# A channel-mixing stage whose GpSimd passes move to TensorE, ScalarE and VectorE

## The reference

```python
a4 = att.reshape(b, l, H, S)
m = jnp.mean(a4, axis=-1, keepdims=True)
var = jnp.mean((a4 - m) ** 2, axis=-1, keepdims=True)
att = ((a4 - m) * jax.lax.rsqrt(var + EPS)).reshape(b, l, E) * gn_w + gn_b
x = x + att * g @ Wo.T
xn2 = _ln(x, ln2_w, ln2_b)
sx2 = _token_shift(xn2, state[:, i0])
xk = xn2 + sx2 * ffn_maa_k
xr = xn2 + sx2 * ffn_maa_r
rr = jax.nn.sigmoid(xr @ ffn_Wr.T)
kk = jnp.square(jax.nn.relu(xk @ ffn_Wk.T))
x = x + rr * (kk @ ffn_Wv.T)
```

## Time and profile before

| what | value |
|---|---|
| time, median of 3 runs | 5353.01 us (5352.04 to 5363.05) |
| profiled execution | 5354.71 us, its span 5352.7 us |
| mean granted TensorE clock | 0.946 |
| busy over the span | PE 4758.5, DVE 3731.0, ACT 2930.4, POOL 2071.8 us |
| the changed stage | from 1351.5 to 1746, 394.5 us |

### The profile page before, as it was taken

How to read it: one execution, slowest core, us unless ns; L and a number is a source line. 1 busy time by engine, 2 the same in 40 slices (tenths; PEclk the granted TensorE clock), 3 DMA queues, 4 the chain that set the end, 5 groups by cost and what they waited for, 6 DMA issues and landing times. The chain is left out here.

```text
span 5352.7 us, 75036 instructions
## 1 busy us (share of the span) xinstructions
PE 4758.5 (89%) x28626; PEld 1687.4 (32%) x28626; DVE 3731.0 (70%) x4661; ACT 2930.4 (55%) x5439; POOL 2071.8 (39%) x924
## 2 busy tenths in 40 slices
PE   5995988999378799997899999997899999996899
PEld 2342433334133233332322222222343333331344
DVE  5658999999565677771599999993457777771431
ACT  2443444444344366664288888885226666665442
POOL 0005666666131388775000000000007888886000
PEclk9997999999699799998999999998999999998999
DMA  2334344343301433323211111112424233221200
GB/s 98 132 117 128 114 109 112 104 114 98 114 32 48 89 69 69 71 58 104 75 29 33 34 34 32 34 30 70 112 75 102 60 68 71 60 49 68 71 24 16
DMA packets 474607, 391.60 MB, mean 73 GB/s; under 512 B 174895, under 2 KB 372372, under 8 KB 474216
## 3 DMA queue, kind: packets, MB, share of 16 engines
q1 hardware_dynamic: 474240, 386.74, 26.7%
HBM read 246.24 MB, written 139.34 MB: 72 GB/s over the span
## 5 line engine op out<-in xcount | busy, mean ns | idle before, releaser
L2941 DVE TENSOR_REDUCE att_part<-att_scores 128x2 f32<-128x802 f32 x1024 | 953.6, 987 | 112.0 <-PE att_scores L2780 100.2
L2914 ACT ACTIVATE att_prob<-att_lower 128x512 f32<-128x512 f32 (+1 forms) x1664 | 883.7, 596 | 132.2 <-PE att_lower L2794 110.9
L3711 DVE TENSOR_REDUCE att_part<-att_scores 128x1 f32<-128x423 f32 x1280 | 676.0, 590 | 240.9 <-PE att_scores L3442 240.7
L3655 ACT ACTIVATE att_prob<-att_lower 128x512 f32<-128x512 f32 (+1 forms) x1088 | 563.2, 602 | 243.9 <-PE att_lower L3454 242.1
L3695 POOL TENSOR_TENSOR att_acc<-att_acc,att_prob 128x1024 f32<-128x1024 f32 (+2 forms) x240 | 671.3, 2797 | 51.6 <-ACT att_prob L3655 22.4
L2517 DVE TENSOR_REDUCE att_part<-att_scores 128x1 f32<-128x401 f32 x1024 | 515.3, 567 | 162.0 <-PE att_scores L2331 161.9
L1511 POOL TENSOR_TENSOR scan_z<-scan_r,scan_states 128x512 f32<-128x512 f32 x256 | 469.7, 1839 | 360.0 <-DVE scan_states L1588 347.9
L2809 PE MATMUL att_lower<-att_prob,att_v 128*32 128x256 f32 (+1 forms) x6144 | 526.0, 415 | 19.7 <-issue 19.7
L2456 ACT ACTIVATE att_prob<-att_scores 128x512 f32<-128x512 f32 (+1 forms) x832 | 430.7, 601 | 195.3 <-PE att_scores L2343 195.3
L2928 POOL TENSOR_TENSOR att_out<-att_sums_sb,att_spread 128x512 f32<-128x512 f32 x32 | 40.7, 1272 | 1170.5 <-DMA att_spread<-recips 1170.5
L2497 POOL TENSOR_TENSOR att_acc<-att_acc,att_prob 128x1024 f32<-128x1024 f32 (+2 forms) x176 | 450.3, 2559 | 68.6 <-ACT att_prob L2456 56.2
(11 more groups left out here) (397 smaller groups left out, 7875.8 us busy)
## 6 DMA issues: line engine op xcount, KB each, us to landing
v<-scan_val SPq DMA_DIRECT2D x96, 256.0 KB, 2.3
att_v<-v SPq DMA_DIRECT2D x32, 768.0 KB
att_spread<-recips SPq DMA_DIRECT2D x64, 256.0 KB
mix_plane<-in_mask SPq DMA_DIRECT2D x16, 800.5 KB, 6.5
att_k<-k1hi SPq DMA_DIRECT2D x32, 400.2 KB
att_k<-k3hi SPq DMA_DIRECT2D x32, 400.2 KB
scan_x<-in_ctx_t SPq DMA_DIRECT2D x12, 1024.0 KB, 6.0
o<-att_out SPq DMA_DIRECT2D x32, 256.0 KB, 2.0
```

The costliest lines, as they stand in the source:

```text
L2914: nc.scalar.activation(prob[g % NP][0:kw(kt), h, :], scores2[0:kw(kt), n % RING2, :], ACT.Exp).then_inc(exped, 1)
L2941: nc.vector.reduce_max(part[q % 2][:, :, ec, piece], scores1[:, bank["unit", p], :, 0:PIECE], AX.X).then_inc(reduced, 1)
L3655: nc.scalar.activation(prob[g % NP][0:kw(kt), h, :], scores2[0:kw(kt), n % RING2, :], ACT.Exp).then_inc(exped, 1)
L3711: nc.vector.reduce_max(part[q % 2][:, hc, piece:piece + 1], scores1[:, bank["piece", p], 0:PIECE], AX.X).then_inc(reduced, 1)
```

## The change

Every GpSimd pass of the stage goes to another engine, and the block of GpSimd is empty.

- VectorE builds `centring`, the identity minus the matrix of head means, and TensorE multiplies it with the heads (`gmean`), so `g` holds the centred heads and no engine subtracts. ScalarE squares `g`, not `att`. The spread 1/std is drained into `att`, and `weigh` multiplies `att` by `g`, now on VectorE in all batches.
- ScalarE squares the keys: once from `kk` into `ms.hi`, then `kk` in place. VectorE's `key_low` waits for the second (`relu2`).
- `weigh`, `apply_gate`, `att_low` and `query_low` are VectorE's, at places of its order given below.
- On ScalarE `rmix_high(b)` follows `mix_high(b)` at once (before, it followed the drains of `value`), `att_high(1)` and `weight_high(4)` follow the casts of `mix(0)`.
- SyncE loads the six vectors and `prev` right after heads 0, ahead of `headrow`, Wo and the gate. TensorE waits for `headrow` at the first `gspread`; ScalarE waits for the vectors at the first affine pass, VectorE at `mix(0)`.

```diff
                 load_att(0)
+                for n in vec:
+                    sp.dma_start(vec[n][:], w[n]).then_inc(small, 16)
+                sp.dma_start(prev[:], w["prev0"].rearrange("b p c -> p b c")).then_inc(small, 16)
                 sp.wait_ge(cleared, 2)
...
                 load_weight(0)
                 load_gate(0)
-                for n in vec:
-                    sp.dma_start(vec[n][:], w[n]).then_inc(small, 16)
-                sp.dma_start(prev[:], w["prev0"].rearrange("b p c -> p b c")).then_inc(small, 16)
...
                 def head_spread(b):
+                    if b == 0:
+                        pe.wait_ge(rows, 16 * C)
                     pe.wait_ge(inverted, b + 1)
...
-                pe.wait_ge(built, 1)
-                pe.wait_ge(rows, 16 * C)
+                pe.wait_ge(built, 2)
...
-                            group([(k["headmean"][:], att[b % 2][:, c, :])])
+                            group([(centring[:], att[b % 2][:, c, :])])
...
                 def head_square(b):
-                    act.wait_ge(gcentred, b + 1)
+                    act.wait_ge(drained, ends[b, "gmean"])
...
-                    nc.scalar.activation(sq[:], att[b % 2][:], ACT.Square).then_inc(gsquared, 1)
+                    nc.scalar.activation(sq[:], g[:], ACT.Square).then_inc(gsquared, 1)
...
                 def key_high(b):
-                    act.wait_ge(relu2, b + 1)
-                    nc.scalar.activation(ms.hi[:], kk[:], ACT.Identity).then_inc(khigh, 1)
+                    act.wait_ge(drained, ends[b, "key"])
+                    nc.scalar.activation(ms.hi[:], kk[:], ACT.Square).then_inc(khigh, 1)
+                    act.wait_ge(khigh, b + 1)
+                    nc.scalar.activation(kk[:], kk[:], ACT.Square).then_inc(relu2, 1)
...
-                act.wait_ge(small, 16 * (len(vec) + 1))
...
                     elif what == "gspread":
-                        act.wait_ge(gcentred, b + 1)
                         for c in part:
-                            drain(g[:, c, :], ACT.Identity)
+                            drain(att[b % 2][:, c, :], ACT.Identity)
                         if b == 0:
+                            act.wait_ge(small, 16 * (len(vec) + 1))
                             affine(0)
...
                         if b == 0:
-                            weight_high(4)
-                            att_high(1)
                             mix_high(0)
                             rmix_high(0)
+                            att_high(1)
+                            weight_high(4)
                         elif b == 1:
                             att_high(2)
                             mix_high(1)
+                            rmix_high(1)
...
-                        if b + 1 < B:
-                            rmix_high(b + 1)
...
                                 mix_high(b + 2)
+                                rmix_high(b + 2)
...
-                centre_heads(1)
-                weigh(1)
-                apply_gate(1)
-                att_low(1)
-                for b in range(B):
-                    square_keys(b)
-                    if b + 2 < B:
-                        centre_heads(b + 2)
-                        weigh(b + 2)
-                        apply_gate(b + 2)
-                    if b:
-                        query_low(b - 1)
-                    if b + 2 < B:
-                        att_low(b + 2)
-                query_low(B - 1)
...
                 def key_low(b):
-                    dve.wait_ge(khigh, b + 1)
+                    dve.wait_ge(relu2, b + 1)
...
+                nc.vector.tensor_tensor(centring[:], k["ident"][:], k["headmean"][:], ALU.subtract).then_inc(built, 1)
...
-                dve.wait_ge(small, 16 * (len(vec) + 1))
-                first_heads()
+                invert_heads(0)
+                weight_low(0)
+                weigh(0)
+                apply_gate(0)
+                att_low(0)
                 weight_low(1)
                 invert_heads(1)
                 weight_low(2)
                 add_residual(0)
                 centre(0)
+                weigh(1)
                 total_squares(0)
                 weight_low(3)
+                dve.wait_ge(small, 16 * (len(vec) + 1))
                 mix(0)
+                apply_gate(1)
+                att_low(1)
                 weight_low(4)
                 for b in range(B):
...
                     key_low(b)
                     if b + 1 < B:
                         centre(b + 1)
+                    if b + 2 < B:
+                        weigh(b + 2)
+                    if b + 1 < B:
                         total_squares(b + 1)
+                    if b + 2 < B:
+                        apply_gate(b + 2)
+                    if b + 1 < B:
                         mix(b + 1)
+                    if b + 2 < B:
+                        att_low(b + 2)
+                    if b:
+                        query_low(b - 1)
                     add_values(b)
                 x_low(B - 1)
+                query_low(B - 1)
```

More of the change, by code:

```diff
@@ L551, in rwkv_outputs @@
         mean, std, gstd = ph.sb("mean", [P, T]), ph.sb("std", [P, T]), ph.sb("gstd", [P, T])
+        centring = ph.sb("centring", [P, P])
         headcol, headrow = ph.sb("headcol", [P, 32]), ph.sb("headrow", [P, P])
@@ L557, in rwkv_outputs @@
         gloaded, cleared, built = ph.sem("gloaded"), ph.sem("cleared"), ph.sem("built")
-        gcentred, gsquared, inverted, weighed, offset, gated, ahigh, alow = (
-            ph.sem(n) for n in ("gcentred", "gsquared", "inverted", "weighed", "offset", "gated", "ahigh", "alow"))
+        gsquared, inverted, weighed, offset, gated, ahigh, alow = (
+            ph.sem(n) for n in ("gsquared", "inverted", "weighed", "offset", "gated", "ahigh", "alow"))
         residual, totalled, centred, squared, mixed, mhigh, mlow, rmixed, rhigh, rlow = (
@@ L930, in total_chunks, with weigh, apply_gate, att_low @@
                     nc.vector.tensor_tensor(tot[:, 0, :], tot[:, 0, :], tot[:, 1, :], ALU.add).then_inc(totalled, 1)
[L932 to L945, removed]
+                def weigh(b):
+                    dve.wait_ge(drained, ends[b, "gspread"])
+                    nc.vector.tensor_tensor(att[b % 2][:], att[b % 2][:], g[:], ALU.mult).then_inc(weighed, 1)
+                def apply_gate(b):
+                    dve.wait_ge(offset, C * (b + 1))
+                    dve.wait_ge(gloaded, 16 * (b + 1))
+                    nc.vector.tensor_tensor(att[b % 2][:], att[b % 2][:], gate[:], ALU.mult).then_inc(gated, 1)
+                def att_low(b):
+                    dve.wait_ge(ahigh, b + 1)
+                    nc.vector.tensor_tensor(as_.lo[:], att[b % 2][:], as_.hi[:], ALU.subtract).then_inc(alow, 1)
+                def query_low(b):
+                    dve.wait_ge(qhigh, b + 1)
+                    nc.vector.tensor_tensor(qs.lo[:], oq[:], qs.hi[:], ALU.subtract).then_inc(qlow, 1)
                 def invert_heads(b):
```

## The result

The changed kernel takes 5308.63 us in the median of four runs (5299.31 to 5308.92), the kernel before beside it 5352.52. The ratio of the runs is 0.9907, 95% interval 0.9891 to 0.9923: 0.9% faster, clear of 1, as forecast. Four runs on each side leave that uncertain by some us: the quotient of the two medians is 0.9918 and would give 5309.1. The sign and the mechanism held; the size was short.

The account below looks back on a forecast made before the run. Bound: each batch's chain, mostly VectorE passes, stretched behind GpSimd. 37.5 us of stretch, 5.7 at the start and 1.8 at the tail, less 7.0 of new waits, made 38.0 off 5354.7: 5316.7, as median 5315; range 5305 to 5327.

Parts of the forecast that it names:

- stretch: Extra length of VectorE's chain passes while standing still behind GpSimd passes; 37.5 us were to go.
- the square and subtraction at the start: Batch 0: the head square starts after the last drain, without a subtraction and two hand-overs; 2.4 us gained.
- the places of `key(0)` and `key(1)`: Starts of the first two key groups, forecast 18.1 and 25.3 us ahead of the recorded ones.
- the reload of x as the new wait before batch 3: Before `key(3)`: x lands 26.1 us after `key(2)` starts, where the residual sum waited to 24.2; 1.9 us lost.
- ScalarE waiting for query_low before it drains `value(1)`: Batch 2: query_low(0), moved to VectorE behind `mix(2)`, puts that drain 9.7 us after the start of `key(2)`.
- the room in PSUM: Undrained `value` holds four banks; `out` stops if the first drain ends over 10.5 us after `key` starts; forecast 10.3, free.
- ScalarE's first drains: Stage start: drains follow the products instead of waiting for the vectors; last drain at 1363.6, 3.3 us ahead.
- rival E: Stage start: heads land no earlier than `headrow` did, Wo late; 2 to 5 us less, 5317 to 5320; within the forecast's 0.68.
- The new waits between `key(0)` and `key(1)`: Losses of 0.8 us for squaring keys twice on ScalarE, 0.4 for `weigh(2)` and 0.4 for `apply_gate(2)`.
- the working for `key(2)`: `value(1)`, moved 25.7 us earlier and without a 1.4 us wait, frees `ms`; the third key group starts 35.9 ahead.
- the bound on TensorE's clock: Before `key(2)` and `key(3)`: if products stay fast after shorter gaps, up to 1.9 us return at each; 0 taken.
- rival C: TensorE's products stay fast over the shorter gaps, or the start is quicker: 5306 to 5311 us; chance 0.10.

Follow-up runs that it names:

- idle passes: Changed kernel plus the 20 old GpSimd passes on a spare tile nobody reads: median 5333.1 us, ratio 0.9964 to the kernel before, stage 384.5 us.
- filler products: Changed kernel plus matrix products, later overwritten, that keep TensorE busy while it waits: ratio 0.9919 to the kernel before, stage 354.2 us, 2.9 shorter than the changed kernel.

## Why the prediction was right and where it failed

Right: that VectorE stands behind GpSimd and that its passes are the chain (37.4 of stretch for 37.5; the long passes are gone, and come back with idle passes). Right too: the square and subtraction at the start, the places of `key(0)` and `key(1)` within 0.5 us, the reload of x as the new wait before batch 3, and ScalarE waiting for query_low before it drains `value(1)`:

```profile
1579.89 0.60 ACT L88 ACTIVATE ffn_oq<-ffn_psum 128x512 f32<-128x512 f32 x1 [6.18 <-DVE ffn_qsl L906]
```

```profile
1596.22 2.29 DVE L915 TENSOR_TENSOR ffn_x<-ffn_x,ffn_o 128x2048 f32<-128x2048 f32 x1 [5.34 <-DMA ffn_x<-in_x_t]
```

Also the room in PSUM: no wait in the changed kernel (the first drain ended 10.0 after `key(2)`, forecast 10.3), one of 2.6 us as soon as it came later. By the rule of the Trainium skill ("Perfetto Trace Analysis", Optimizing Scalar/DVE Operations) that a saturated VectorE may hand work even to GpSimd, the change should have lost up to 29.8 us; the stage got 42.7 shorter. VectorE wasn't saturated here (228 of 400 us), so the rule is not refuted. Its caveat, that handing work between these two might not help because they share a port, agrees with the idle passes, which show the standstill (3.03 for a copy of 0.17); that it is a port no run here can show.

Small misses: ScalarE's first drains were 2.8 ahead, not 3.3, since the heads land no earlier than `headrow` did (rival E, half true, 0.5 us). The new waits between `key(0)` and `key(1)`, put at 1.6, took some 0.8. In the working for `key(2)` the product `value(1)` is moved by 25.7, while `key(1)` in front of it is 25.3 ahead; nothing there gives the 0.4. And the steps add up to 37.3 of stretch and 6.8 of waits, not 37.5 and 7.0, with the same 38.0.

The step that failed is the bound on TensorE's clock. I moved the recorded lengths of TensorE's groups along unchanged, wrote that up to 1.9 us might come back at `key(2)` and `key(3)`, and took 0. The groups on the chain in fact ran as follows: `key(1)` 12.94 before and 12.09 after (0.9); the head squares and first gates of batch 1 1.93 and 5.89, then 1.06 and 5.36 (1.4); `key(2)` 12.39 and 12.23 (0.2); `key(3)` 12.07 and 10.54 (1.5). These lengths run from the first product's start to the last one's end. The granted clock over the first 4 us from the head squares and of `key(3)`, in the kernel before:

```profile
1560.50:1564.50 4.00, 3.98 (x16) 1.08 (x17) 3.61 (x4) 1.92 (x2) 0.00 (x0) 0.62 0.00 0
...
1672.90:1676.90 4.00, 3.91 (x11) 1.48 (x12) 4.00 (x8) 2.76 (x5) 0.00 (x0) 0.59 0.00 0
```

In the changed kernel both stretches have 1.00. The four gains are 3.9 us; against them the first `out` (12.67 for 12.39) and `key(0)` (12.11 for 11.80) lost 0.6, and the last query gained 0.1. So the clock gave 3.5 of the 4.7 us that the stage won beyond 38.0. Of the rest, some 1.2, about 1.0 came between `key(0)` and `key(1)`, most of it from the smaller waits, and 0.4 between `key(2)` and `key(3)`. That the clock is a term of its own the filler products show; this division of the 4.7 is read from the two traces and was not tested by itself. I looked for the clock only behind the two gaps that I had computed, not behind every gap that the change shortens. It was rival C with its 4 to 9 us, at 0.10, and it should have been part of the forecast. The range was also too narrow by a second thing. The stage's 42.7 alone would make 5310.3, inside it; what carries 5303.2 out lies outside the stage, in the drift of the others, some 5 us in a single execution, for which it had no room.

The new place of `rmix_high` was not tried by itself: at the old place, behind the drain of `value(1)`, it would wait for query_low(0), which stands on VectorE behind `mix(2)`, which waits for `rmix_high(2)`, and the engines would wait for each other in a circle. It belongs to the move of query_low. What stays open: why the same gap of 3.25 us is followed by the one clock or the other. It did not go by the gap's length here, and the second execution of the changed kernel agreed with the first.

## What to carry to other kernels

Before an elementwise pass is given to GpSimd, look at VectorE's shortest and longest instance of one and the same form. If they differ by up to the length of a GpSimd pass and the long ones end with or just behind one, the pass isn't free but is paid by VectorE, and moving it to VectorE itself can be a gain. Taking work off GpSimd pays only where VectorE's stall is on the chain, and which passes those are changes with the schedule. Where the groups behind a wait on TensorE are part of the chain, count them at both clocks, and shorten the wait and keep TensorE busy together, for each alone may give its gain back.

## What was not expected of the hardware

A one-input 128x4 copy of 0.17 us took up to 4.0 us beside a GpSimd pass, held until that pass ended just as a pass over 2048 elements is; its size did not matter. It holds the other way too: an idle GpSimd pass of 3.60 took 5.71 beside a VectorE subtraction. VectorE's reciprocal alone, always begun before the GpSimd pass it met, was never longer than 3.35. GpSimd's pass takes 3.60 when both inputs are one tile and 4.50 with two (float32, undisturbed). TensorE behind 3.25 us of idleness was granted 1.00, 0.65, 0.66, 0.58, 1.00 or 0.50 of its clock over the next 4 us; of these the changed kernel's two were profiled twice, 0.65 then 0.66, and 1.00 both times.
